# Recurrent stage: the receptance product and the residual sum on POOL from a halved receptance

## The reference

```python
x_prev = jnp.concatenate([x[:, :1], x[:, :-1]], axis=1)
kvr = _layernorm(x, g1, b1) @ W_tm
k, v, r = jnp.split(kvr, 3, axis=-1)
k = k * tmk + x_prev * (1.0 - tmk)
v = v * tmv + x_prev * (1.0 - tmv)
r = jax.nn.sigmoid(r * tmr + x_prev * (1.0 - tmr))   # the receptance
y, new_state = _wkv(time_decay, time_first, k, v)    # the recurrence over 256 steps
x = x + r * y                                        # the product and the residual sum
xp = jnp.concatenate([x[:, -1:], x[:, :-1]], axis=1)
xn = _layernorm(x, g2, b2)
kk = (xn @ W_cm) * cmk4 + xp4 * (1.0 - cmk4)
rr = jax.nn.sigmoid(xn * cmr + xp * (1.0 - cmr))
x = x + rr * (jnp.square(jax.nn.relu(kk)) @ W_cp)
```

## Time and profile before

| | us |
|---|---|
| median of 3 runs | 717.51 (716.87 to 718.19) |
| the profiled execution, whole | 717.23 |
| its span in the trace | 715.3 |
| PE busy | 673.5 (94%) |
| DVE busy | 570.0 (80%) |
| ACT busy | 417.0 (58%) |
| POOL busy | 324.5 (45%) |

### The profile page before, as it was taken

One profiled execution on the slowest core, in us unless ns is written; L12 is line 12 of the kernel. 1 busy time (PEld: TensorE's weight loads), 2 busy tenths in 40 slices (PEclk: granted clock), 3 DMA queues, 4 the chain that ended last, 5 costly groups with the idle time before them and its releaser, 6 DMA issues. The chain is left out here.

```text
span 715.3 us, 12389 instructions
## 1 busy us (share of the span) xinstructions
PE 673.5 (94%) x4100; PEld 501.9 (70%) x4100; DVE 570.0 (80%) x1310; ACT 417.0 (58%) x755; POOL 324.5 (45%) x404
## 2 busy tenths in 40 slices
PE   7899998697899999999999988999999998999997
PEld 5677774543467777777778676777777775777785
DVE  5899978889979888987989867676766676879774
ACT  4657676885246555555656666555565654555554
POOL 2668873101227766456757543220413200545463
PEclk9999999999999999999999999999999999999999
DMA  6636420000014233212313000000000000323231
GB/s 173 200 102 181 161 84 1 0 1 1 1 47 133 71 108 90 90 59 75 104 58 92 30 1 1 2 3 1 2 1 0 0 2 1 120 74 119 61 119 44
DMA packets 34329, 43.16 MB, mean 60 GB/s; under 512 B 5216, under 2 KB 17504, under 8 KB 34272
## 3 DMA queue, kind: packets, MB, share of 16 engines
q1 hardware_dynamic: 34272, 42.46, 19.3%
HBM read 41.13 MB, written 1.31 MB: 59 GB/s over the span
## 5 line engine op out<-in xcount | busy, mean ns | idle before, releaser
L697 POOL TENSOR_TENSOR p_prod<-p_p,p_gate_row 128x512 f32<-128x512 f32 x128 | 204.0, 1605 | 105.7 <-DVE p_p L504 62.3
L384 ACT ACTIVATE p_sil<-p_ps_a 128x512 f32<-128x512 f32 x176 | 105.3, 598 | 131.9 <-PE p_ps_a L100 127.0
L509 DVE TENSOR_TENSOR p_hlo<-p_prod,p_hhi 128x512 fp32r<-128x512 f32 x176 | 149.5, 851 | 0.3 <-ACT p_hhi L393 0.2
L504 DVE TENSOR_TENSOR p_p<-p_sil,p_ps_b 128x512 f32<-128x512 f32 x128 | 87.0, 680 | 51.8 <-ACT p_sil L384 37.3
L393 ACT CAST p_hhi<-p_prod 128x512 fp32r<-128x512 f32 x176 | 108.1, 615 | 21.8 <-POOL p_prod L697 21.8
L98 PE MATMUL p_ps_a<-xt_hi,w_uphi 128*128 128x512 f32 x176 | 74.2, 422 | 0.0
L98 PE MATMUL p_ps_acc<-p_hhi,w_downhi 128*128 128x512 f32 x176 | 71.0, 404 | 1.2 <-DVE p_hlo L509 1.0
L98 PE MATMUL p_ps_b<-xt_hi,w_uphi 128*128 128x512 f32 x176 | 71.1, 404 | 0.1
L100 PE MATMUL p_ps_a<-xt_hi,w_uplo 128*128 128x512 f32 x176 | 70.1, 398 | 0.0
L99 PE MATMUL p_ps_a<-xt_lo,w_uphi 128*128 128x512 f32 x176 | 70.1, 398 | 0.0
L100 PE MATMUL p_ps_b<-xt_hi,w_uplo 128*128 128x512 f32 x176 | 69.9, 397 | 0.0
(11 more groups left out here) (356 smaller groups left out, 1421.4 us busy)
## 6 DMA issues: line engine op xcount, KB each, us to landing
p_gate_row<-gate_rows SPq DMA_DIRECT2D x128, 256.0 KB, 3.3
w_rawbuf<-in_L_ffn_fc_w_dram SPq DMA_DIRECT2D x3, 512.0 KB, 6.2
w_rawbuf<-in_L_ffn_w_dram SPq DMA_DIRECT2D x3, 512.0 KB, 5.7
out_dram<-x SPq DMA_DIRECT2D x4, 256.0 KB, 3.6
w_rawbuf<-in_L_ffn_shared_w_dram SPq DMA_DIRECT2D x3, 256.0 KB, 3.9
x<-in_L_attn_x_dram SPq DMA_DIRECT2D x2, 256.0 KB, 3.8
x<-in_L_attn_x_dram SPq DMA_DIRECT2D x1, 512.0 KB, 8.5
mb_xraw<-in_L_attn_W_B_dram SPq DMA_DIRECT2D x1, 512.0 KB, 5.0
```

The costliest lines, as they stand in the source:

```text
L384: nc.scalar.activation(sil[:, u % 2], ps_a[:, u % 2], ACT.Silu).then_inc(c["sil"].sem, 1)
L504: nc.vector.tensor_tensor(dst, sil[:, u % 2], ps_b[:, u % 2], ALU.mult).then_inc(c["p1"].sem, 1)
L509: nc.vector.tensor_tensor(hlo[:, u % R], prod[:, u % R], hhi[:, u % R].bitcast(F32), ALU.subtract).then_inc(c["hlo"].sem, 1)
L697: G.tensor_tensor(prod[:, u % R], p1[:, u % 2], gate_row[:, e % ROWS], ALU.mult).then_inc(c["prod"].sem, 1)
```

## The change

`received` and `residual` leave DVE's list and go to POOL's. [...] DVE's `parts(m)` for m of 2 and 3 gets a wait for x2 of block m - 2, because POOL may still be reading the buffer `t1` or `t2` that it overwrites.

```diff
             def parts(m):
                 h = m % 2
                 dve.wait_ge(c["r_g"].sem, c["r_g"].at(m + 1))
+                if m >= 2:
+                    dve.wait_ge(c["r_x2"].sem, c["r_x2"].at(m - 1))
                 V.tensor_scalar(t1[h][:], gam[h][:], 0.0, None, ALU.min)
...
-            def received(m):
-                h = m % 2
-                dve.wait_ge(c["r_y"].sem, c["r_y"].at(m + 1))
-                dve.wait_ge(c["r_tr"].sem, c["r_tr"].at(m + 1))
-                V.scalar_tensor_tensor(out=t1[h][:], in0=gate_of(m), scalar=1.0, in1=t2[h][:], op0=ALU.add,
-                                       op1=ALU.mult).then_inc(c["r_p"].sem, 1)
-
-            def residual(m):
-                h = m % 2
-                dve.wait_ge(c["r_p"].sem, c["r_p"].at(m + 1))
-                if m >= 2:
-                    dve.wait_ge(c["r_ot"].sem, c["r_ot"].at(m - 1))
-                V.scalar_tensor_tensor(out=mid(x2[h]), in0=seqs(t1[h][:]), scalar=0.5, in1=mid(y0[h]), op0=ALU.mult,
-                                       op1=ALU.add).then_inc(c["r_x2"].sem, 1)
...
+            def halved(m):
+                pool.wait_ge(c["r_tr"].sem, c["r_tr"].at(m + 1))
+                G.tensor_scalar(gate_of(m), gate_of(m), 0.5, 0.5, ALU.mult, ALU.add).then_inc(c["r_half"].sem, 1)
+
+            def received(m):
+                h = m % 2
+                pool.wait_ge(c["r_half"].sem, c["r_half"].at(m + 1))
+                pool.wait_ge(c["r_y"].sem, c["r_y"].at(m + 1))
+                G.tensor_tensor(t1[h][:], gate_of(m), t2[h][:], ALU.mult).then_inc(c["r_p"].sem, 1)
+
+            def residual(m):
+                h = m % 2
+                pool.wait_ge(c["r_p"].sem, c["r_p"].at(m + 1))
+                if m >= 2:
+                    pool.wait_ge(c["r_ot"].sem, c["r_ot"].at(m - 1))
+                G.tensor_tensor(mid(x2[h]), seqs(t1[h][:]), mid(y0[h]), ALU.add).then_inc(c["r_x2"].sem, 1)
...
             scale(3)
+            halved(0)
+            received(0)
+            residual(0)
+            halved(1)
             scale2(0)
+            received(1)
+            residual(1)
             scale2(1)
+            halved(2)
+            received(2)
+            residual(2)
             scale2(2)
+            halved(3)
+            received(3)
+            residual(3)
             scale2(3)
```

More of the change, by code:

```diff
@@ L1466, in _ @@
             output(0)
-            received(0)
             lead2(1)
-            residual(0)
             parts2(1)
@@ L1477, in _ @@
             output(1)
-            received(1)
-            residual(1)
             wrap(1)
@@ L1512, in _ @@
             shift(6)
-            received(2)
             add_out(0)
-            residual(2)
             lead2(3)
@@ L1528, in _ @@
             output(3)
-            received(3)
-            residual(3)
             shift(8)
@@ L1593, in rwkv_phase @@
     per = {"r_kk": 4, "r_kx": 4, "r_sq": 4, "r_vv": 4, "r_c1": 2, "r_c3": 2}
+    c["r_half"].base += NBLK
     once = {"r_prep": 1, "r_om": 1, "r_uw": 1, "r_vec": 1}
@@ L2439, in program @@
         counts.update({n: Count(sem(n)) for n in RWKV_SEMS})
+        counts["r_half"] = Count(sem("r_half"))
         counts.update({n: counts[spent] if spent else Count(sem(n)) for n, spent in zip(MAMBA_SEMS, SPENT)})
```

## The result

| | before | after |
|---|---|---|
| median of 5 runs, us | 717.94 (716.87 to 720.02) | 721.54 (719.53 to 723.61) |
| ratio | | 1.0043, 95% interval 1.0024 to 1.0063 |
| span of the profiled execution | 715.3 | 719.6 |

A forecast was written before the change was run, and what follows sets the result against it. It took DVE as the bound in the stage's second half, and the chain `output` to `measure2` wherever DVE has nothing else. 1.5 + 0.7 - 0.1 + 0.5 + 0.75 = +3.35 us gave 720.8 us, range 718.2 to 722.9.

The forecast's parts named there:

- Where the chain decides: From `output` to `measure2` in blocks 0, 1 and 3, DVE lacks other work; two POOL instructions take 2.75 us undisturbed.
- The sizes: POOL's product and sum were each taken as 1.27 us undisturbed, with 0.08 us between dependent POOL instructions.
- the hold of the scan: In block 3, `halved(3)` on POOL starts just ahead of `numerators(3)` on DVE and holds it about 0.5 us.
- the delay of block 0's sum: The first half of `parts2(1)` on DVE holds the port about 0.3 us, so `residual(0)` starts on POOL at 132.95.
- Block 0: `measure2(0)` comes 1.5 us later, with `lead2(1)` and `parts2(1)` delaying POOL; 0.8 us later if undisturbed.
- Block 2: POOL delays `square(5)` by 0.70 us, then `add_out(0)`, `shrink(4)` and the transposes wait; net -0.1 us, or -0.8 without interference.
- `halved`: Each one-input halving on POOL takes 0.65 us; those of the first three blocks cost nothing.
- DVE as the bound: Rival, 8%: POOL's work is hidden and eight DVE instructions come back whole, -4.9 us, giving 712.6 us.
- sign of being right: In the recurrent stage, DVE's busy time falls by about 5 us while the stage grows by about 3 us.
- No interference: Rival, 14%: POOL's two-input instructions cost 1.27 us but DVE is not held; +1.5 us, 719.0 us.
- POOL at 1.04: Rival, 11%: POOL's two-input instructions take 1.04 us, as in a narrow form; 718.3 us, no measurable change.
- The clock: Rival, 12%: PE's clock falls to 1.2 GHz between x2(1) and `shift(0)`, adding 1.2 us, giving 722.0 us.

The follow-up runs named there:

- with one block: Product and sum on POOL in block 2 alone, on DVE as in the kernel before elsewhere: stage 86.74 us, 0.18 shorter; 718.65 against 718.76 us, ratio 0.9991.
- with three: Product and sum on POOL in blocks 0, 1 and 3, on DVE in block 2: stage 2.37 us longer than the kernel before; 721.43 us, ratio 1.0028.
- with a shorter chain: Changed kernel without the product by the receptance, one POOL sum per block: stage 85.82 us, 1.10 shorter than the kernel before; 717.35 against 718.24 us, ratio 0.9979.
- the second set: Unaltered changed kernel timed again, 12 runs beside 35 of the kernel before: 720.35 against 718.76 us, ratio 1.0017 (0.9997 to 1.0037).
- the second trace of the changed kernel: Changed kernel profiled once more without any edit: stage 90.65 us, 3.73 longer than in the kernel before.

## Why the prediction was right

| distance in the stage, us | before | after | measured | forecast |
|---|---|---|---|---|
| start to `measure2(0)` | 18.05 | 19.07 | +1.02 | +1.5 |
| `output(1)` to `shift(0)` | 5.20 | 5.75 | +0.55 | +0.7 |
| `output(2)` to `measure2(2)` | 5.85 | 5.63 | -0.22 | -0.1 |
| `measure2(2)` to `output(3)` | 7.05 | 7.25 | +0.20 | +0.5 |
| `output(3)` to `measure2(3)` | 3.44 | 4.02 | +0.58 | +0.75 |
| all that is left | | | +0.05 | 0 |
| the stage | 86.92 | 89.10 | +2.18 | +3.35 |

- *Where the chain decides.* Right in place and sign at each of the four blocks, and shown by the kernels with one block, with three, and with a shorter chain.
- *The sizes.* The product took the 1.27 us that was taken from the FFN stages. The sum took 1.09, not 1.27, 0.12 to 0.18 too much in each of blocks 0, 1 and 3 (in block 0 it took 1.15). Of the 1.17 us by which the forecast of 3.35 exceeds the measured 2.18, this is about 0.45; the hold of the scan is 0.30, the delay of block 0's sum 0.24, block 2 0.12. The estimated 0.08 between dependent POOL instructions was measured: 134.99 - 134.91.
- *Block 0.* `lead2(1)` did delay the product, by 0.31. That the first half of `parts2(1)` would delay the sum by 0.24 was wrong: the sum started at 134.99 and took 1.15. The two halves of `parts2(1)` were the ones that waited, and nothing behind them was late by that. The forecast's 0.8 us for a `parts2(1)` that is not held is too low: it leaves out the delay of the product by `lead2(1)`, for which the earlier trace rows already stood. With that delay the sum gives 1.2.
- *Block 2.* The chain from `square(5)` to `add_out(0)`, `shrink(4)` and the transposes was there as described; without it the gain is 0.9 instead of 0.2. That a DVE instruction with one input in PSUM is not held is read from a row that the earlier trace rows doesn't show, and which stands in the same trace: it runs beside POOL's product of 228.01 to 229.63 and takes its usual time.

```profile
228.40 0.68 DVE L504 TENSOR_TENSOR p_prod<-p_sil,p_ps_b 128x512 f32<-128x512 f32 x1
```

- *`halved`.* 0.62 to 0.80 us against the 0.65 taken. It held the scan for 0.19, not 0.5. The place was right (0.28 us ahead of the scan, 0.23 in the forecast); from the scan's start to the end of `halved(3)` it was 0.34 us, and of that the scan lost only 0.19.
- *DVE as the bound* fell: of the 4.9 us of eight instructions taken away, 3.3 came back as longer instructions (busy 79.1 instead of 80.6), and its idle time in the stage rose from 6.3 to 10.0 us. The forecast's own sign of being right, DVE busy about 5 us less, failed by this: the holds that it had put into the chain were not put into DVE's busy time.
- *No interference* fell: `parts2` was seen held. *POOL at 1.04* was near for the sum alone.
- *The clock* was a rival at 12% with +1.2 us on top. It is no rival but an addition that comes in some executions. Where it fell on the steps named in the forecast it cost 1.6 instead of 1.2, and it did so in two of the seven traces with product and sum of blocks 0 and 1 on POOL. The stage's own growth of 2.2 lies under the forecast of 3.35, and what came on top in the first set was no part of the forecast: the profiled execution grew by 4.1 us (717.23 to 721.33), of which 2.3 stand ahead of the stage. In the second set the medians differ by only 1.6. That the forecast of 720.8 comes so close to the median of 721.54 is in part luck; the place and the sign in each block are not.

## What to carry to other kernels

An engine's busy share says little of what an instruction on it is worth. Look at what stands behind the instruction in its list until the next wait that depends on it: where that is shorter than the time on the slower engine, moving the instruction loses, and where it is longer, it gains, as far as this kernel's four blocks show. Move in the blocks with cover alone, and put instructions that don't meet the other engine's access into the time in which it works. Where an edit makes a gap on PE longer, look at several traces, because a fall of the clock there comes in some executions only.

## What was not expected of the hardware

- On POOL the sum over 128x2x256 takes 1.09 us and the product over 128x512 takes 1.27, undisturbed, both float32 with two inputs from SBUF. Whether the operation or the shape makes this was not tried.
- DVE's tensor_scalar, with one input, is held by POOL: 1.38 and 1.31 us, against 0.43 and 0.42 away from it. By the Trainium skill (SBUF — State Buffer, section "Who interferes with whom") such an instruction can run in a two-port mode and then meets GpSimd; the trace agrees.
- In ten meetings of DVE and POOL over 128x512 in the changed kernel's stage the one that started second lost the time to the end of the first, less 0.13 to 0.15 us, and both engines are found as the second one. Beside DVE instructions with one input in PSUM nothing was lost: the product of block 2 started 0.51 us ahead of the end of such a one (`shift(5)`) and took its 1.27.
- The clock fell to the lower level without a long idle time of PE: in the second trace of the changed kernel no idle time of PE in the 8 us before the fall was over 1.30 us. Filling one gap (28 fillers instead of 12) didn't prevent a fall that cost 1.6 us.
